# Moving the weight loads, the unpacking and block 0's scaling at the seam between cross-attention and the feed-forward net

## The reference

```python
def reference(x, ctx, mask, g_norm, null_kv, Wq, Wkv, Wout, g_out, k0, k1, k2, s0, s1, s2):
    # cross-attention, 16 heads of 64
    h = layer_norm(_layernorm(x), g_norm)
    q = h @ Wq
    k, v = split(ctx @ Wkv)
    k, v = [null_k; k], [null_v; v]            # 1602 keys
    out = softmax(mask(q @ k.T / 8)) @ v       # per head
    x = x + layer_norm(out @ Wout, g_out)
    # feed-forward net; the weights are booleans that stand for +1 and -1
    y = _layernorm(x)
    h = concat([y, -y])                        # 512 columns
    h = relu(s0 * (h @ pm1(k0))) * 2           # 512 -> 1024
    h = relu(s1 * (h @ pm1(k1))) * 2           # 1024 -> 1024
    return x + s2 * (h @ pm1(k2))              # 1024 -> 256
```

## Time and profile before

| | |
|---|---|
| median of 3 runs | 1440.07 us (1439.2 to 1440.87) |
| profiled execution, its own time | 1440.29 us |
| span, first to last instruction | 1438.5 us |
| mean granted clock of TensorE | 0.992 |
| busy: TensorE | 1383.4 us, 96% of the span |
| busy: GpSimd | 989.1 us, 69% |
| busy: VectorE | 705.0 us, 49% |
| busy: ScalarE | 627.0 us, 44% |

### The profile page before, as it was taken

How to read it: one execution, slowest core, us unless ns; L and a number is a source line. 1 busy time by engine, 2 the same in 40 slices (tenths; PEclk the granted TensorE clock), 3 DMA queues, 4 the chain that set the end, 5 groups by cost and what they waited for, 6 DMA issues and landing times.

```text
span 1438.5 us, 21039 instructions
## 1 busy us (share of the span) xinstructions
PE 1383.4 (96%) x7972; PEld 773.8 (54%) x7972; DVE 705.0 (49%) x972; ACT 627.0 (44%) x760; POOL 989.1 (69%) x498
## 2 busy tenths in 40 slices
PE   7999999999999999999999999999988987999998
PEld 3345455545545555555455545545544635877876
DVE  5445554554454555455554545454546264444542
ACT  4334445444444444444445444544443342233232
POOL 1027889889988988898889889988988775110100
PEclk9999999999999999999999999999999998999999
DMA  5240001000100010010001000100050220102000
GB/s 150 75 141 1 16 16 46 16 16 16 53 16 16 22 47 16 16 47 16 16 16 46 16 15 16 54 16 16 16 166 8 75 74 23 59 15 73 0 15 15
DMA packets 54992, 53.74 MB, mean 37 GB/s; under 512 B 13745, under 2 KB 41332, under 8 KB 54900
## 3 DMA queue, kind: packets, MB, share of 16 engines
q1 hardware_dynamic: 54900, 52.50, 11.7%
HBM read 34.79 MB, written 17.56 MB: 36 GB/s over the span
## 4 chain that ended last, share of the span: by engine, by line
PE 83%; ACT 8%; DVE 3%; POOL 2%; issue 2%; DMA 1%; SPq 1%; DVEq 0%; ACTq 0%; POOLq 0%
PE ps_o L1335 25%; PE ps_s L1322 19%; ACT prob L816 7%; PE ps_x L1424 7%; PE ps_x L1202 7%; PE ps_s L1424 4%; PE ps_o L1255 4%; PE ps_s L1202 3%; PE ps_s L1386 3%; POOL acc L647 2%; PE ps_o L1272 2%; PE ps_s L1188 2%; PE ps_o L1244 2%; PE ps_o L1246 2%; PE ps_s L1190 1%
## 5 line engine op out<-in xcount | busy, mean ns | idle before, releaser
L647 POOL TENSOR_TENSOR acc<-acc,prob 128x1024 f32<-128x1024 f32 x352 | 838.3, 2382 | 100.1 <-ACT prob L816 56.6
L968 DVE TENSOR_REDUCE mxh<-ps_x 128x2 f32<-128x804 f32 x408 | 406.8, 997 | 515.3 <-PE ps_x L1202 515.2
L816 ACT ACTIVATE prob<-ps_s,keybias 128x1024 f32<-128x1024 f32 x416 | 440.6, 1110 | 280.4 <-PE ps_s L1322 279.7
L1335 PE MATMUL ps_o<-prob,vp 128*64 128x512 f32 x1664 | 404.9, 608 | 1.4 <-DMA vp<-v_scratch 1.4
L1335 PEld LDWEIGHTS ps_o<-prob,vp 128*64 128x64 f32 x1664 | 101.2, 136 | 175.7 <-issue 167.3
L1202 PE MATMUL ps_x<-kh,qh 64*128 64x402 f32 x816 | 164.0, 397 | 9.7 <-DVE mxh L968 9.0
L1202 PEld LDWEIGHTS ps_x<-kh,qh 64*128 64x128 f32 x816 | 77.3, 185 | 165.7 <-issue 87.4
L1322 PE MATMUL ps_s<-ql,kh 64*128 64x512 f32 x832 | 165.5, 392 | 0.0
L1322 PE MATMUL ps_s<-shift,one_sel 64*128 64x512 f32 x832 | 165.2, 392 | 0.0
L1322 PE MATMUL ps_s<-qh,kh 64*128 64x512 f32 x832 | 164.9, 392 | 0.0
L1322 PE MATMUL ps_s<-qh,kl 64*128 64x512 f32 x832 | 164.6, 391 | 0.0
(11 more groups left out here) (149 smaller groups left out, 1201.5 us busy)
## 6 DMA issues: line engine op xcount, KB each, us to landing
rb<-r_scratch SPq DMA_DIRECT2D x64, 128.0 KB, 2.9
o_scratch<-o_sb SPq DMA_DIRECT2D x32, 256.0 KB, 2.0
otb<-o_scratch SPq DMA_DIRECT2D x4, 2048.0 KB, 8.0
v_scratch<-vsb SPq DMA_DIRECT2D x13, 512.0 KB, 3.2
vp<-v_scratch SPq DMA_DIRECT2D x8, 832.0 KB, 5.0
xs<-in_x SPq DMA_DIRECT2D x4, 512.0 KB, 6.8
xres<-in_x SPq DMA_DIRECT2D x1, 2048.0 KB, 13.0
out<-obuf SPq DMA_DIRECT2D x8, 256.0 KB, 2.1
```

What stands on the lines that cost most here:

```text
L647: gp.tensor_tensor(a, so_far, term, ALU.add).then_inc(sums_p, 1)
L816: act.activation(prob[:, slot(u, s), :, :], ps_s[s % S_BUFS][:, :, :], ACT.Exp, bias=keybias[:, kt:kt + 1], scale=SCALE).then_inc(p_made, 1)
L968: dve.reduce_max(mxh[:, :, qt, quarter], ps[:, :, 0:MXW], AX.X).then_inc(x_free, 1)
L1335: last = pe.matmul(ps_o[qb % 2][rows(g), :], vp[u][:, kt, rows(g)], prob[:, slot(u, s), g, :], start=(kt == 0), stop=(kt == KT - 1))
```

## The change

- The transfers of the byte weights, `gout` and `wo_sb` are issued by ScalarE, at cycle 22 of pair 6, and that of `xres` at cycle 1 of the last pair, each with its own semaphore. The tiles are laid out anew so that their places are free then; `w1` becomes eight tiles.
- `shift` becomes two tiles of 512 columns, one for even and one for odd blocks of all pairs; `set_shift` waits until the scores of two blocks earlier are made.
- `w1` is unpacked by ScalarE, a tile a cycle from 6 to 13 of the last pair. `w0` is unpacked by VectorE in four pieces at cycle 17. `w2` is unpacked by ScalarE in two halves inside layer 1 of block 0.
- Block 0 is scaled by ScalarE (with the negated mean times the inverse root as bias) at cycles 21 and 24. VectorE's steps between stand at cycle 22, the multiplication with `gout` in one operation. GpSimd's first roots come after the third query block's additions, the second ones after the seventh addition of the fourth.
- TensorE transposes block 0 before the last two steps of values, into `ps_x`. ScalarE and VectorE make `yhi` and `ylo` in two halves of 256 rows, without the wait for GpSimd's last addition.
- Block 0's pass through `tail` is written out on TensorE and ScalarE, and holds the sums of the last block (before tile 2 of layer 1); VectorE inverts and normalises them at tiles 5 and 7.

```diff
@@ SyncE @@
-            def set_shift(n, u, qb):
-                sp.wait_ge(row_made, blocks(n, qb) + 1)
+            def set_shift(n, qb):
+                b = blocks(n, qb)
+                sp.wait_ge(row_made, b + 1)
+                if b >= 2:
+                    sp.wait_ge(s_made, KT * (b - 1))
                 for g in range(2):
-                    sp.dma_start(shift[u][g * HD:g * HD + 1, qb * QW:(qb + 1) * QW].bitcast(F32),
+                    sp.dma_start(shift[qb % 2][g * HD:g * HD + 1, :].bitcast(F32),
                                  rowbuf[qb % 2][4 * g:4 * g + 4, :].bitcast(F32)).then_inc(shift_set[qb], 16)
...
-                    sp.dma_start(k0raw[:, :, :], k0.rearrange("(c p) n -> p c n", p=P)).then_inc(ld_raw, 16)
...
-                    sp.dma_start(gout[:, :], g_out.unsqueeze(0).broadcast_to([P, DIM])).then_inc(ld_tail, 16)
@@ GpSimd @@
+            def root_of_block_0(r):
+
+                gp.wait_ge(y0_var, 2 + r)
+                gp.tensor_scalar(y0var[r][:, :], y0mv[r][:, :, 1], EPS, None, ALU.add).then_inc(y0_root, 1)
+                gp.tensor_scalar(y0nm[r][:, :], y0mv[r][:, :, 0], -1.0, None, ALU.mult).then_inc(y0_root, 1)
+                gp.wait_ge(y0_root, 4 * r + 1)
+                gp.tensor_tensor(y0rs[r][:, :], y0var[r][:, :], minus_half[:, :], ALU.pow).then_inc(y0_root, 1)
+                gp.wait_ge(y0_root, 4 * r + 3)
+                gp.tensor_tensor(y0nm[r][:, :], y0nm[r][:, :], y0rs[r][:, :], ALU.mult).then_inc(y0_root, 1)
...
                         add(n, u, qb, i)
+                        if last and qb == 3 and i == 7:
+                            root_of_block_0(1)
...
+                    if last and qb == 2:
+                        root_of_block_0(0)
...
-                    for k in range(FK):
-                        gp.tensor_scalar(w1[:, k, :], k1raw[:, k, :], 2.0, -1.0, ALU.mult, ALU.add).then_inc(w1_made, 1)
@@ ScalarE @@
+            def load_ffn_weights():
+                act.wait_ge(k_lo, 4 * PAIRS)
+                act.wait_ge(q_lo, QB * PAIRS)
+                act.dma_start(k0raw[:, :, :], k0.rearrange("(c p) n -> p c n", p=P)).then_inc(ld_raw, 16)
+                act.dma_start(k2raw[:, :, :], k2.rearrange("(c p) n -> p c n", p=P)).then_inc(ld_raw, 16)
+                act.dma_start(k1raw[:, :, :], k1.rearrange("(c p) n -> p c n", p=P)).then_inc(ld_raw, 16)
+                act.dma_start(gout[:, :], g_out.unsqueeze(0).broadcast_to([P, DIM])).then_inc(ld_gout, 16)
+                act.dma_start(wo_sb[:, :, :], wout.rearrange("(c p) n -> p c n", p=P)).then_inc(ld_wo, 16)
+
+            def scale_block_0(r):
+
+                act.wait_ge(y0_root, 4 * (r + 1))
+                for t in range(4):
+                    act.activation(y0[:, t, :], (xres if r else y0)[:, t, :], ACT.Identity, bias=y0nm[r][:, t:t + 1],
+                                   scale=y0rs[r][:, t:t + 1]).then_inc(y0_scaled, 1)
...
+                    if n == PAIRS - 2 and c == 22:
+                        load_ffn_weights()
+                    if last and c == 1:
+                        act.wait_ge(pv_done, RING + STEPS * n)
+                        act.dma_start(xres[:, :, :], x[0].rearrange("(t p) d -> p t d", p=P)).then_inc(ld_res, 16)
+                    if last and 6 <= c < 6 + FK:
+                        act.wait_ge(ld_raw, 48)
+                        act.activation(w1[c - 6][:, :], k1raw[:, c - 6, :], ACT.Identity, bias=minus_one[:, :], scale=2.0).then_inc(w1_made, 1)
+                    if last and c == 21:
+                        scale_block_0(0)
+                    if last and c == 24:
+                        scale_block_0(1)
                 if last:
+                    for h in range(2):
+                        act.wait_ge(t_made, 2 * h + 2)
+                        act.activation(yhi[:, :, 2 * h * P:(2 * h + 2) * P], ps_x[:, h, :].rearrange("p (c q) -> p c q", c=DC),
+                                       ACT.Copy).then_inc(yhi_made, 2)
                     copy_o(n, QB - 1, False)
...
+                    if start and m == 2:
+                        last_sums()
+                    if start and m in (3, 4):
+                        half = slice(4 * (m - 3), 4 * (m - 2))
+                        act.activation(w2[:, half, :], k2raw[:, half, :], ACT.Identity, bias=minus_one[:, :], scale=2.0).then_inc(w2_made, 1)
@@ VectorE @@
-                for t in range(4):
-                    dve.tensor_scalar(y0[:, t, :], y0[:, t, :], y0mv[0][:, t, 0:1], y0rs[0][:, t:t + 1],
-                                      ALU.subtract, ALU.mult).then_inc(y0_step, 1)
...
+                dve.wait_ge(y0_scaled, 4)
+                dve.wait_ge(ld_gout, 16)
+                dve.wait_ge(ld_res, 16)
+                dve.tensor_tensor(y0[:, :, :], y0[:, :, :], gout[:, :].unsqueeze(1).broadcast_to([P, 4, DIM]), ALU.mult).then_inc(y0_step, 1)
...
+            def split_small_weights():
...
+                for q in range(4):
+                    cols = slice(q * DIM, (q + 1) * DIM)
+                    dve.tensor_tensor(w0[:, :, cols], k0raw[:, 0:DC, cols], k0raw[:, DC:2 * DC, cols], ALU.subtract).then_inc(w0_made, 1)
...
-            dve.wait_ge(pv_done, RING + STEPS * PAIRS)
-            dve.wait_ge(sums_p, 1 + SUMS_P * QB * PAIRS)
-            for i in range(4):
-                rest_of_y(0, i)
+            for h in range(2):
+                dve.wait_ge(yhi_made, 2 * h + 2)
+                dve.tensor_tensor(ylo[:, :, 2 * h * P:(2 * h + 2) * P], ps_x[:, h, :].rearrange("p (c q) -> p c q", c=DC),
+                                  yhi[:, :, 2 * h * P:(2 * h + 2) * P].bitcast(F32), ALU.subtract).then_inc(y_split, 2)
...
+                if start:
+                    dve.wait_ge(sums_p, 1 + SUMS_P * (QB * PAIRS - 1) + freed_by(7))
                 for j in range(2, 8):
                     split(b, j)
...
+                if start:
+                    dve.wait_ge(sums_p, 1 + SUMS_P * QB * PAIRS)
+                for j in range(8):
+                    if start and j == 5:
                         invert(PAIRS - 1, 3, False)
@@ TensorE @@
+            def turn_block_0():
+
+                pe.wait_ge(x_free, x_count(X_LAST, LAST_PAIR))
+                pe.wait_ge(y0_scaled, 8)
+                for t in range(4):
+                    for c in range(DC):
+                        last = pe.transpose(ps_x[:, t // 2, (2 * c + t % 2) * P:(2 * c + t % 2 + 1) * P],
+                                            y0[:, t, c * P:(c + 1) * P], ident[:, :])
+                    last.then_inc(t_made, 1)
...
                 if last:
+                    turn_block_0()
                     for s in (STEPS - 2, STEPS - 1):
                         values(n, u, s, plan, pair)
...
+                    if start and m == 2:
+                        pe.wait_ge(y_job_free, y_count(Y_LAST, LAST_PAIR))
+                        pe.wait_ge(o_copied, QB * PAIRS)
+                        sums(ps_last, PAIRS - 1, QB - 1)
                     if with_next:
                         chain(b + 1, m)
```

More of the change, by code:

```diff
@@ L218, in xattn_ffn_kernel @@
         one_sel = sb("one_sel", [P, P], F32R)
+        shift = [sb(f"shift{r}", [P, QW], F32R) for r in range(2)]
         s8, r8 = sb("s8", [P, 8]), sb("r8", [P, 8])
@@ L236, in xattn_ffn_kernel @@
         operands(0)
-        shift.append(sb("shift0", [P, SEQ], F32R))
+        at["spent"] = at["raw"] = end_spent = at[""]
         xT = sb("xT", [P, DC, SEQ])
@@ L270, in xattn_ffn_kernel @@
         assert at["head"] <= end_head
[L273 to L277 removed]
+        k0raw = sb("k0raw", [P, 2 * DC, FF], U8, region="spent")
+        k1raw = sb("k1raw", [P, FK, FF], U8, region="spent")
+        k2raw = sb("k2raw", [P, FK, DIM], U8, region="spent")
+        gout = sb("gout", [P, DIM], region="spent")
+        wo_sb = sb("wo_sb", [P, PAIRS, DIM], region="spent")
+        hf = [sb(f"hf{r}", [P, QW], region="spent") for r in range(2)]
+        assert at["spent"] <= end_tail0, (at["spent"], end_tail0)
         xres = sb("xres", [P, QT, DIM], region="tail0")
[L279 removed]
         w0 = sb("w0", [P, DC, FF], F32R, region="tail0")
[L281 to L283 removed]
+        w1 = [sb("w1_0", [P, FF], F32R, region="tail0")]
         cst = [sb(f"cst{r}", [P, 2, 6], region="tail0") for r in range(2)]
@@ L308, in xattn_ffn_kernel @@
         y0var = [sb(f"y0var{r}", [P, 4], region="vp0") for r in range(2)]
+        y0nm = [sb(f"y0nm{r}", [P, 4], region="vp0") for r in range(2)]
         y0rs = [sb(f"y0rs{r}", [P, 4], region="vp0") for r in range(2)]
@@ L1052, in body @@
                         maxima(j, job, pair, ps_s[0])
+                    if last and c == C_AT[0]:
+                        split_small_weights()
                     for j, i in plan[c]["C"]:
@@ L1057, in body @@
                             invert(n - 1 if qb == 3 else n, qb, first and qb == 0)
-                    if last and c == 21:
+                    if last and c == 22:
                         attn_block_0()
-                    if last and c == 24:
```

(18 more changed lines are left out.)

144 lines of the change are left out of this document (62 added, 82 removed).

## The result

The changed kernel takes 1424.8 us (median of 4 runs, 1423.91 to 1425.88) against 1440.5 for the one before on the same chip: a ratio of 0.9891, 95% interval 0.9873 to 0.9908, or 15.7 us less. The forecast was 1,421.6 with a range of 1,414 to 1,431: right in sign and within the range, 3 us too low. The profiled execution took 1424.45 us, span 1422.2, so 16.3 us less span.

The account below looks back on a forecast made before the run. TensorE, 83% of the span, was taken as the bound, losing time in two last-pair waits and at the seam. 5.1 + 6.5 + 9.7 - 2.8 = 18.5 us saved gave 1,421.6 us, range 1,414 to 1,431.

Parts of the forecast that it names:

- The first wait: Last pair, TensorE's wait up to 1,066.09 us: moving the weights off SyncE's queue removes it, 5.1 us won.
- The second: Last pair, TensorE's wait up to 1,101.56 us: taking VectorE's unpacking of `w0` and `w2` from cycle 10 wins 6.5 us.
- The four pieces at cycle 17: `w0` on VectorE during its wait for the attention output product: at most 13.5 us, pushing only the first statistics by 2.
- ScalarE's issues: Pair 6, cycle 22: five transfers take ScalarE 4.8 us and delay exponentials, costing 2.8 us, range 0 to 9.2.
- `gout` blocks ScalarE: Rival, pair 6: `gout` holds ScalarE as it did SyncE, costing 9.2 us instead of 2.8; 1,428.0 us, chance 0.12.
- The rival that traffic was the trouble: Pair 6 or early last pair: TensorE waits again, the 5.1 us are not won; 1,426.7 us, chance 0.08.
- Table loads: Rival: ScalarE's Identity operations for `w1` and block 0's scalings reload function tables, 17 to 34.5 us lost; chance 0.06.
- The seam: Last attention values to layer 1: earlier scaling and transposing of block 0 starts layer 1 earlier, 9.7 us net, 4.2 to 15.2.
- the lateness of the exponentials: Seam: last exponentials 3.1 us late behind block 0's second scaling; the forecast fails if held longer than 3 us.
- the seam is held by GpSimd: Rival: layer 0 starves until GpSimd's additions end and the clock falls, 4.2 us instead of 9.7; 1,427.1 us, chance 0.07.
- Moving the transposes ahead of the last values: Seam: block 0 transposed early, last values end 1.9 us later, layer 0's first product starts at 1,184.8 us.

Follow-up runs that it names:

- experiment 4: Changed kernel with all six transfers back on SyncE's queue at the start of the last pair, in the old order: 1426.7 us.
- experiment 7: Changed kernel with VectorE's four pieces of `w0` at cycle 10 instead of 17: 1437.3 us.
- experiment 8: Changed kernel with block 0 transposed after the last values instead of before the last two steps of them: 1424.8 us.
- experiment 5: Changed kernel with ScalarE's five issues in pair 6 parted, three byte tensors at cycle 22, `gout` and `wo_sb` at cycle 24: 1420.8 us.
- experiment 1: Changed kernel with GpSimd's second inverse roots of block 0 after its fifth addition of the last query block instead of its seventh: 1422.8 us.
- experiment 2: Changed kernel without GpSimd's last five additions of the last query block, so some softmax sums are incomplete: 1417.3 us.
- experiment 6: Changed kernel with GpSimd's second roots after the fifth addition and VectorE taking the sixth to tenth addition of the last query block: 1416.2 us.
- experiment 3: Changed kernel with `gout` issued by SyncE at the start of the last pair instead of by ScalarE in pair 6: 1423.7 us.

## Why the prediction came out as it did

*The first wait (5.1 us):* right, 5.1; experiment 4 brought it back, with 7.6 us in its profiled execution and less by its median. *The second (6.5 us):* right, 6.5; experiment 7, with `w0` alone but in four pieces, brought back 9.7. The four pieces at cycle 17 took 11.07 us where 13.5 was the bound, under a TensorE product.

*ScalarE's issues (2.8 us, range 0 to 9.2):* 2.0 us in the changed kernel's profile. That figure is one draw: over the kernels that keep the group it is 1.6 to 4.7, so that 2.8 was not wrong. The issues took 4.4 us and not 4.8, but I had `gout` at 0.44 and `wo_sb` at 2.10, and it was the other way round. The rival "`gout` blocks ScalarE" was right in its place and wrong in its size: whatever is fourth waits, by all the times on record until the first has landed. I charged half a fall of the clock; the clock stood at 1.00 after this 1.62 us wait, and was 0.72 in the six us from 1,031 in experiment 8, where the wait was 2.78 us.

*The rival that traffic was the trouble* did not come about: the 5.1 us were won and the sums came back in time. But its mechanism is not refuted, since the change took these sums away from the issuing and from the traffic at once, and no run parts the two. In the kernel before the store of the sums was issued at 1,057.55 and their load only at 1,063.40:

```profile
1057.55 0.57 SPq L486 DMA_DIRECT2D s_scratch<-s_sb  x2
```

That is 5.85 us (6.5 in experiment 4), where the next block has 1.46. So some 4.4 us of the lateness came after the issuing of the weights was over, while 348 GB/s were still moving (1,058 to 1,062). The Trainium skill (DMA: Bandwidth & Descriptors, Issuing engines are not separate DMA queues) says that transfers from different issuers run on the same DMA engines and interleave. The trace agrees: beside the weights in pair 6, 3.95 us passed from the store of the inverted sums (1,034.15, SyncE's queue) to the load of them (1,038.10), against 1.5 us otherwise, and 6.7 us in experiment 5. Nothing waited for it.

*Table loads:* none; the eight `w1` operations took 1.15 us each.

*The seam (9.7 us net, range 4.2 to 15.2):* this is the term of the sum that was mis-sized: 6.7 us (7.9 less 1.2). The mechanism was the one forecast, but two sizes were short. GpSimd's additions took 2.77 us each on average and not 2.47 beside VectorE's two wide operations, which I had delayed by GpSimd but not the reverse, and the scaling took 2.07 us and not 1.6: the last exponentials were 5.3 us late, not 3.1, and GpSimd ended at 1,183.1, 1.7 us after my 1,191.0 less the 9.6 us of lead. That makes the third ReLU 1.2 us late. From it to layer 1 it took 11.0 us, not 8.05 and 1.3, because the clock was low for longer. The first of the two is firm: the third ReLU stands within 0.1 us of the same place in all five kernels with this seam. The second is partly chance: it was 8.9 to 10.3 us in the other four, on both sides of my 9.35. Experiment 1 shows that the lateness of the exponentials, which I had named as what would break the forecast, is not what held the seam, and experiment 8 that the start of layer 0 isn't either; experiments 2 and 6 show that the additions are. The rival "the seam is held by GpSimd" thus described the trace well (layer 0 starved and the clock fell), but its 4.2 us was as far from 6.7 as the forecast's 9.7 (2.5 and 3.0 us), and its 1,427.1 from 1424.8.

*Moving the transposes ahead of the last values* gave nothing measurable as it stands: 2.1 of the 3.5 us that it hides are covered by the wait for the additions, and the rest is within the spread of the seam.

## What to carry to other kernels

When a serial tail is cut, look for the engine that is still finishing earlier work, and count its operations twice: for the time until it ends, and for what each of them does to a neighbour that alternates with it. Give that rest to an engine that does it alone and fast, and only then move the start of the next stage forward. On an engine's queue issue few transfers at a time, the next ones when the first have landed.

## What the runs showed of the hardware

- A 128x1024 addition took GpSimd 2.36 to 2.39 us alone. Beside such additions VectorE operations with two SBUF inputs were slow: 0.69 us of work became about 2.2, 1.22 us (128x1024) became 3.20 and 3.30, and pieces of 512 byte columns took 2.4 to 2.8. The additions slowed as well: six beside the two wide operations took 16.60 us, 2.3 more than alone. The two halves of `ylo`, with one input in PSUM, took 1.29 us beside them and 1.29 in experiment 2, without additions. A cast with a single SBUF input was slow too: 1.99 us beside them (2.58 in experiment 1), 0.43 without.
- The Trainium skill (SBUF — State Buffer, Who interferes with whom) says that a VectorE instruction with two SBUF inputs contends with a GpSimd instruction that reads SBUF, and that one with at most one SBUF input does not, except in the modes that use both ports, which copies, casts and `tensor_scalar` can enter. The trace agrees for `h0lo`, `w0` and `ylo`. The slow casts, and the four scalings of 2.5 us each in the kernel before, fit the exception, but no run here shows in which mode they ran.
- The fourth transfer of a group on ScalarE's queue took 2.01 to 3.35 us to issue, whichever it was, and ended about when the first had landed (3.9 to 4.6 us after its issue); that the landing is the cause is read from this coincidence alone. Transfers issued after that took 0.35 to 0.46 us. On SyncE's queue `gout`, sixth, took 5.88 and 5.89 us; alone, in experiment 3, 0.43.
- The granted clock of TensorE stood at 1.00 after the waits of 1.62 and 2.77 us in the changed kernel, and averaged 0.65 in the six us with the end of its 2.88 us wait and one of 1.04 us. It averaged 0.66 in the five us after the waits of 3.23 and 4.60 us in the kernel before. After waits of 2.78 us it averaged 0.72 in experiments 2 and 3 (1,172 to 1,178), 0.75 in 5 (1,171 to 1,177) and 0.72 in 8 (1,031 to 1,037). So the length of the last wait alone does not tell what the clock does: 2.77 us left it up in the changed kernel, and 2.78 us brought it down in four others.
